# Scan constants and first chunks kept in tensors across stages, and the gate product one pair later in the second scan

## The chip, the cores and the metric

One core of one Trainium2 chip. The metric is the device time of the whole kernel in microseconds, the median of the runs.

## The reference

```
x = x + tanh(g_xattn) * SSM(ctx, layernorm(x))
x = x + tanh(g_ffn)  * Layer(layernorm(x))

# SSM, per batch of 1024 tokens and 1024 channels, 16 states per channel
u = silu(conv4(in_proj_w @ ctx) + conv_b)
dt_lo, B, C = split(x_proj_w @ u)
delta = softplus(dt_proj_w @ dt_lo + dt_proj_b)
state[t] = state[t-1] * exp(delta[t] * A) + delta[t] * u[t] * B[t]
y[t] = sum_n state[t, n] * C[t, n] + D * u[t]
y = y * silu(z)

# Layer: only the 128 tokens of a batch that a router scores highest (of all four batches: 512 rows)
h = rms_norm(rows); causal attention, 16 heads; MLP silu(h @ w_gate) * (h @ w_up) @ w_down
```

There are four batches; x is 4 x 1024 x 1024 and all is in float32.

## The kernel before

The kernel runs seven stages, one after the other: `project_stage`, `scan_stage(0)`, `route_stage(0)`, `layer_stage(0)`, `scan_stage(2)`, `route_stage(2)`, `layer_stage(2)`. The number is the first batch of the pair that the stage handles. Each stage has tensors and semaphores of its own, which are given back when it ends, and it ends with a barrier of all engines. SP waits, as a stage's last act, for the DMAs that it and ACT issued in it.

**Projection (line 59).** 32 steps, one for each batch and each of 8 groups of 128 channels (`e`). PE multiplies the context by in_proj, VectorE runs the convolution and ACT the silu; ACT stores the group's u and its gate input (silu of the normed x, 1 MB together) to a scratch tensor `ug` (line 194), and each batch's dt, B and C rows to a scratch tensor `xd` (line 202). SP loads x tile after tile (`load_x`, line 110), each when the tile before has been used.

**Scan (line 278).** The work is 32 units: 2 batches x 2 halves of 512 tokens (a chunk is one batch's half) x 8 channel groups. A unit has 16 states, in 8 pairs and 4 quads:

- ACT, `exp(delta * A)`, two per pair, into the PSUM ring `pA` (line 773). It also copies the transposed result of the unit before, `copy_x2`, from PSUM (line 698) at pair `X2_AT` = 4, and turns the gate (line 694).
- POOL, quads `x = du * bB` (line 531), and for pairs 2 and 5 the product with C (line 538), 
- VectorE, the 16 scans (line 823), the products with C for the other pairs (line 808), and the gate product (line 797) for the unit before. Its place is after pair `GATE_AT` = 1; it waits for PE's last sum of the unit before (`summed`) and for the turned gate.
- PE, sums of the states over pairs by products with the identity (line 592) into the PSUM tile `py`, the skip D * u (line 586, a product with the diagonal `diagD`), which for unit s begins when the gate product of s-1 has read `py`, and the product that adds x (lines 581 and 582). In program order it is skip(s), sums of pair 0, pair 1, then the add of unit s-1.
- SP loads `bB` (B of a chunk, broadcast to 128 partitions, 4 slices of 1 MB, line 421), `bC` (line 434), `dt` (412), `u` (386), the gate input and x (394, 398).

At its start the stage loads tanh inputs, `ssm`, `w_dt`, then dt, u, B and C of its first chunk; it makes the identity on POOL, tanh and the diagonals on ACT (line 765), and `negA`, minus the exp of A_log.

In the second scan (`fill=True`) PE also computes gate, up and down products of the MLP of the first pair of batches, between its sums, from a ring of four weight tiles (line 442), and VectorE and ACT carry its activations (lines 829 to 841). PE's order is fixed, so a product whose weights are late holds all that stands behind it.

**Layer (line 1127).** PE multiplies the selected rows with tiles of weights of 512 KB that SP loads into a ring of `SLOTS_W` = 8 slots, in the order wq 16 tiles, wk 8, wv 8 (from tile `T_V` = 24), wo 16 (line 1240). A tile's load waits until the tile whose slot it takes has been used. The DMA queue of SP works in order.

Some constants of the scan stage:

```
GATE_AT, ADD_AT, TURN_AT, DT_AT = 1, 1, 3, 5
READ_AT, X2_AT, COPY_AT = 1, 4, 6
```

Of the kernel before, what the change touches and what calls it, by code (L numbers as in the profile page):

```python
# [24 lines left out]
P = 128  # L25
# [33 lines left out]
def project_stage(nc, t, ctx):  # L59
# [31 lines left out]
    exponent = sem("exponent")  # L91

    with nc.Block() as block:
        @block.sync
        def _(sp):
# [73 lines left out]
        def _(act):  # L169
# [91 lines left out]
GATE_AT, ADD_AT, TURN_AT, DT_AT = 1, 1, 3, 5  # L261
# [16 lines left out]
def scan_stage(nc, t, ctx, first, fill):  # L278
# [10 lines left out]
    bB = sb("bB", [P, NS, HALF])  # L289
    bC = sb("bC", [P, NS, HALF])  # L290
# [19 lines left out]
    g_in, small, made, act_chain, consts = (sem(n) for n in ("g_in", "small", "made", "act_chain", "consts"))  # L310
# [1374 lines left out]
```

## Time and profile before

| | us |
|---|---|
| median of 3 runs | 3162.67 |
| lowest and highest | 3158.97, 3163.16 |
| the profiled execution | 3152.81 |
| its span (first to last instruction) | 3151.1 |

| engine | busy us | share of the span |
|---|---|---|
| PE (TensorE, products) | 2432.4 | 77% |
| VectorE (DVE) | 2176.0 | 69% |
| POOL (GpSimd) | 1668.0 | 53% |
| ACT (ScalarE) | 1288.0 | 41% |

The mean granted clock of PE is 0.858 of full. A profile gives the time of one execution; its span is 1.7 us short of that execution's time. The busy share is an average over seven stages with different limits, so it is read stage by stage: the rows below give the busy time of each engine in windows that begin and end with the stages. A row of the timeline says when an instruction began, how long it took, and in brackets how long its engine was idle before it and what ended that.

### The profile page before, as it was taken

The numbers are of one execution on the slowest core, as the hardware profiler recorded it, in microseconds if no ns is written. First come the engines' busy times: TensorE is split into PE (matmuls) and PEld (weight loads), VectorE is DVE, ScalarE is ACT, GpSimd is POOL, SyncE is SP. The second block draws the span as 40 slices with busy tenths as digits, with TensorE's granted clock in tenths as the row PEclk, the third lists the DMA queues.
The fourth block names the chain that finished last, engine by engine and source line by source line (L and its number), as shares of the span: only waits on it lengthen the run. The fifth ranks groups of instructions, "written<-read, shape, count | busy, mean of one in ns | idle before, by whom it ended". The sixth has DMA issues, their size and how long they took to land. (4 is left out here: it accounts for less than half of the span.)

```text
span 3151.1 us, 30288 instructions
## 1 busy us (share of the span) xinstructions
PE 2432.4 (77%) x10552; PEld 1700.3 (54%) x10552; DVE 2176.0 (69%) x2674; ACT 1288.0 (41%) x2311; POOL 1668.0 (53%) x601
## 2 busy tenths in 40 slices
PE   8996667666666632998488888888887179999998
PEld 3332555554545521854366676665554166658863
DVE  5664999999999985331599999999997832410000
ACT  4555555555555522131456555555543211510000
POOL 0001999999999941000688988899996000000000
PEclk9998677777777765999699998899998589999999
DMA  7545314114141134423623632633531564044443
GB/s 283 191 186 202 89 40 148 41 41 149 47 135 55 37 124 185 127 87 98 213 85 99 208 101 80 204 105 109 185 101 60 211 211 134 15 147 151 151 152 107
DMA packets 198094, 401.37 MB, mean 127 GB/s; under 512 B 16960, under 2 KB 85056, under 8 KB 192832
## 3 DMA queue, kind: packets, MB, share of 16 engines
q1 hardware_dynamic: 186752, 343.43, 34.8%
q10 hardware_dynamic: 9856, 51.38, 4.0%
q0 software_dynamic: 1344, 4.72, 0.4%
q8 instruction: 82, 1.34, 0.2%
q14 instruction: 60, 0.49, 0.0%
HBM read 323.98 MB, written 75.50 MB: 127 GB/s over the span
## 5 line engine op out<-in xcount | busy, mean ns | idle before, releaser
L531 POOL TENSOR_TENSOR s_x<-s_du,s_bB 128x2048 f32<-128x2048 f32 x256 | 1156.9, 4533 | 116.6 <-PE s_py L592 93.6
L592 PE MATMUL s_py<-s_ident,s_x 128*128 128x128 f32 x4096 | 668.4, 322 | 363.9 <-DVE s_x L808 351.7
L592 PEld LDWEIGHTS s_py<-s_ident,s_x 128*128 128x128 f32 x4096 | 583.2, 169 | 535.5 <-DVE s_x L808 431.8
L773 ACT ACTIVATE s_pA<-s_delta,s_negA 128x512 f32<-128x512 f32 x1024 | 666.1, 680 | 388.0 <-DVE s_x L808 381.7
L823 DVE TENSOR_TENSOR_SCAN s_pA<-s_pA,s_x 128x512 f32<-128x512 f32 x384 | 452.4, 1214 | 66.9 <-POOL s_x L531 46.7
L823 DVE TENSOR_TENSOR_SCAN s_pA<-s_pA,s_carry,s_x 128x512 f32<-128x512 f32 x384 | 471.6, 1270 | 0.1
L808 DVE TENSOR_TENSOR s_x<-s_pA,s_bC 128x1024 f32<-128x1024 f32 x384 | 461.9, 1203 | 1.0 <-DMA s_bC<-scratch_xd 0.9
L1324 PE MATMUL l_p<-l_hT,l_ring 128*128 128x256 f32 x1792 | 396.7, 380 | 1.8 <-ACT l_hT L1428 1.0
L1324 PEld LDWEIGHTS l_p<-l_hT,l_ring 128*128 128x128 f32 x1792 | 341.7, 191 | 49.5 <-issue 1.4
L538 POOL TENSOR_TENSOR s_x<-s_hp,s_bC 128x1024 f32<-128x1024 f32 x128 | 301.6, 2356 | 12.0 <-DVE s_hp L823 12.0
L1292 POOL TENSOR_TENSOR l_squares<-l_squares,l_minus_half 128x1 f32<-128x1 f32 x4 | 2.2, 554 | 494.6 <-DVE l_squares L1583 494.6
L151 PE MATMUL p_x<-p_ctxT,p_w_in 128*128 (+1 forms) x512 | 231.0, 604 | 9.4 <-DMA p_ctxT<-in_ctxT 9.3
L1331 PE MATMUL l_p<-l_ring,l_hidden 128*128 128x512 f32 x512 | 220.2, 592 | 0.0
L239 DVE SCALAR_TENSOR_TENSOR p_ug<-p_raw,p_conv,p_ug 128x1024 f32<-128x1024 f32 x96 | 123.3, 1285 | 87.1 <-ACT p_ug L185 78.5
L1301 POOL DMA_INDIRECT out_dram<-l_rows,l_row_i x2 | 1.9, 951 | 330.5 <-DVE l_rows L1610 330.5
L712 ACT ACTIVATE s_carry<-s_pA 128x2 f32<-128x2 f32 x192 | 33.1, 172 | 343.4 <-DVE s_x L808 343.4
L151 PEld LDWEIGHTS p_x<-p_ctxT,p_w_in 128*128 128x128 f32 x512 | 95.7, 192 | 143.4 <-issue 142.5
L1331 PEld LDWEIGHTS l_p<-l_ring,l_hidden 128*128 128x128 f32 x512 | 97.1, 190 | 121.1 <-issue 121.0
L823 DVE TENSOR_TENSOR_SCAN s_hp<-s_pA,s_carry,s_x 128x512 f32<-128x512 f32 x128 | 162.4, 1269 | 0.0
L125 POOL TENSOR_TENSOR p_rstd<-p_mv,p_minus_half 128x1 f32<-128x1 f32 x32 | 18.4, 575 | 262.4 <-DVE p_mv L234 262.4
L1605 DVE TENSOR_TENSOR l_hidden<-l_silu,l_p 128x256 f32<-128x256 f32 x32 | 13.5, 421 | 207.8 <-PE l_p L1324 207.8
L823 DVE TENSOR_TENSOR_SCAN s_hp<-s_pA,s_x 128x512 f32<-128x512 f32 x128 | 154.5, 1207 | 0.1
(177 smaller groups left out, 3034.8 us busy)
## 6 DMA issues: line engine op xcount, KB each, us to landing
scratch_ug<-p_ug ACTq DMA_DIRECT2D x32, 1024.0 KB, 3.9
s_bB<-scratch_xd SPq DMA_DIRECT2D x32, 1024.0 KB, 13.1
s_bC<-scratch_xd SPq DMA_DIRECT2D x32, 1024.0 KB, 14.0
p_xz<-in_x SPq DMA_DIRECT2D x32, 512.0 KB, 3.5
s_u<-scratch_ug SPq DMA_DIRECT2D x64, 256.0 KB, 3.6
s_gy<-scratch_ug SPq DMA_DIRECT2D x64, 256.0 KB, 4.2
s_xt<-in_x SPq DMA_DIRECT2D x64, 256.0 KB, 4.6
scratch_x<-s_xt SPq DMA_DIRECT2D x64, 256.0 KB, 4.3
```

What stands on the lines that cost most here:

```text
L125: pool.tensor_tensor(out=rstd[:, e % 2:e % 2 + 1], in0=mv[:, e % 2, 1:2], in1=minus_half[:], op=ALU.pow).then_inc(rstd_ready, 1)
L151: last = nc.tensor.matmul(halves(ps[e % 2], h), w_in[:, c, e * P:(e + 1) * P], ctxT[:, bass.ds((b * NK + c) * L + h * HALF, HALF)], start= ...
L239: nc.vector.scalar_tensor_tensor(out=ug[:, j, 0], in0=raw[:, j, i:i + L], scalar=conv[:, e, i:i + 1], in1=ug[:, j, 0], op0=ALU.mult, op1=A ...
L531: pool.tensor_tensor(out=x[:, 4 * g:4 * g + 4], in0=du[:, s % 2:s % 2 + 1].broadcast_to([P, 4, HALF]), in1=bB[:, 4 * g:4 * g + 4], op=ALU. ...
L538: pool.tensor_tensor(out=x[:, 2 * i:2 * i + 2], in0=hp[:, POOL_PAIRS.index(i)], in1=bC[:, 2 * i:2 * i + 2], op=ALU.mult).then_inc(pool_hc, 1)
L592: last = nc.tensor.matmul(py[:, a], x[:, n, a * P:(a + 1) * P], ident[:], is_transpose=True, start=False, stop=is_last and a == HALF // P - 1)
L712: nc.scalar.activation(kept, pA[:, j:j + 2, HALF - 1], ACT.Copy).then_inc(carried, 1)
L773: nc.scalar.activation(pA[:, n % 4], delta[:, s % 2], ACT.Exp, scale=negA[:, s % NE, n:n + 1]).then_inc(dA_ready, 1)
L808: nc.vector.tensor_tensor(x[:, 2 * i:2 * i + 2], pA[:, j:j + 2], bC[:, 2 * i:2 * i + 2], ALU.mult).then_inc(vec_hc, 1)
L823: nc.vector.tensor_tensor_scan(out, pA[:, n % 4], x[:, n], initial, ALU.mult, ALU.add).then_inc(scanned, 1)
L1324: last = nc.tensor.matmul(out[:, 0:ROWS], w[:, c * P:(c + 1) * P], src[:, c], start=c == 0, stop=c == KT - 1)
L1331: last = nc.tensor.matmul(banks[2 * a + h][:], src[:, a * P:(a + 1) * P], w[:, h * HALF:(h + 1) * HALF], start=is_first, stop=is_last)
```

## The change

Three parts.

1. A class `Kept` holds B, C, dt, u of one chunk, and the constants `ssm`, `w_dt`, `negA`, `diagD`, the identity and tanh(g), in tensors that live over the first five stages. `project_stage` loads the constants (after its first x loads), makes the identity and the diagonals, and after its last x load issues 11 loads of the first chunk: u twice (256 KB each), dt (64 KB), B and C (8 x 1 MB). SP waits for them at the end of the stage.
2. `layer_stage(0)` issues the same 11 loads for batch 2, after the load of tile 24. For the room its ring has 6 slots, not 8, and four of its work tensors share one. `scan_stage` has no loads, waits or making of constants at its start any more; its first loads are the gate input and x, and in the second scan then h2T, the coefficients and the weight ring. `negA` is computed in the first scan alone.
3. `GATE_AT` becomes (1, 2): in the second scan the gate product stands after pair 2.

```diff
+class Kept:
...
+    def load_units(self, sp, t, b, sem):
+        for e in range(2):
+            sp.dma_start(self.u[:, e], t["ug"][(b * NE + e) * P:(b * NE + e + 1) * P, 0:HALF]).then_inc(sem, 16)
+
+    def load_chunk(self, sp, t, b, sem):
+        sp.dma_start(self.dt[:, 0], t["xd"][b * ND:b * ND + NR, 0:HALF]).then_inc(sem, 16)
+        for g in range(NS // 4):
+            for dst, at in ((self.bB, b * ND + NR + 4 * g), (self.bC, b * ND + NR + NS + 4 * g)):
+                sp.dma_start(dst[:, 4 * g:4 * g + 4], t["xd"][at:at + 4, 0:HALF].partition_broadcast(P)).then_inc(sem, 16)
...
             with sp.Fori(1, NB) as b:
                 load_x(b, 0)
+            for e in range(2):
+                sp.wait_ge(ug_out[e], 16 + 16)
+            keep.load_units(sp, t, 0, kept)
+            sp.wait_ge(xd_out, 32 + 32)
+            keep.load_chunk(sp, t, 0, kept)
+            sp.wait_ge(kept, 16 * KEPT_LOADS)
             sp.wait_ge(xd_out, 32 * NB + 32)
...
             batch(0, True)
+            act.wait_ge(small, 48)
+            act.wait_ge(made, 2)
+            nc.scalar.activation(keep.tg[:], keep.tg[:], ACT.Tanh).then_inc(kept_chain, 1)
+            for e in range(NE):
+                last = nc.scalar.activation(keep.diagD[:, e], keep.ident[:], ACT.Copy, scale=keep.ssm[:, e, NS + 1:NS + 2])
+            last.then_inc(kept_chain, 1)
...
-GATE_AT, ADD_AT, TURN_AT, DT_AT = 1, 1, 3, 5
+GATE_AT, ADD_AT, TURN_AT, DT_AT = (1, 2), 1, 3, 5
...
-            sp.dma_start(tg[:], t["g"].partition_broadcast(P)).then_inc(g_in, 16)
-            sp.dma_start(ssm[:], t["ssm"].rearrange("(e p) c -> p e c", p=P)).then_inc(small, 16)
-            sp.dma_start(w_dt[:], t["w_dt"].rearrange("(e r) c -> r e c", r=NR)).then_inc(small, 16)
-            load_dt(0)
-            load_u(0)
-            load_B(0, 0)
-            load_C(0, 0)
-            load_u(1)
-            for g in range(1, QUADS):
-                load_B(0, g)
-                load_C(0, g)
             load_end(0)
...
-                    if i == GATE_AT and s:
+                    if i == GATE_AT[fill] and s:
                         gate(s - 1)
...
-    SLOTS_W = 8
+    SLOTS_W = 8 if last_half else 6
...
             for n in range(SLOTS_W, TILES):
                 load(n)
+                if n == T_V and not last_half:
+                    keep.load_units(sp, t, SPAN, kept)
+                    keep.load_chunk(sp, t, SPAN, kept)
```

VectorE's order in the second scan, pairs 0 to 3 of one unit (`s_pA` and `s_hp` are the outputs of scans, `s_x` the states' products with C, `s_gy` the gate's output). Before:

```order
L823 SCALAR_TENSOR_TENSOR s_pA<-s_pA,s_x 128x512 [waits s0_dA_ready]
L808 TENSOR_TENSOR s_x<-s_pA,s_bC 128x1024 [waits s0_scanned]
L823 SCALAR_TENSOR_TENSOR s_pA<-s_pA,s_x 128x512 [waits s0_dA_ready]
L797 TENSOR_TENSOR s_gy<-s_py,s_gy 128x512 [waits s0_gate_turned,s0_summed]
L823 SCALAR_TENSOR_TENSOR s_hp<-s_pA,s_x 128x512 [waits s0_pool_hc,s0_carried,s0_dA_ready,s0_w_ready]
L808 TENSOR_TENSOR s_x<-s_pA,s_bC 128x1024 [waits s0_scanned]
L823 SCALAR_TENSOR_TENSOR s_hp<-s_pA,s_x 128x512 [waits s0_dA_ready]
L823 SCALAR_TENSOR_TENSOR s_pA<-s_pA,s_x 128x512 [waits s0_dA_ready] x2
```

Changed:

```order
L841 SCALAR_TENSOR_TENSOR s_pA<-s_pA,s_x 128x512 [waits p_kept_chain]
L826 TENSOR_TENSOR s_x<-s_pA,k_bC 128x1024 [waits s0_scanned]
L841 SCALAR_TENSOR_TENSOR s_pA<-s_pA,s_x 128x512 [waits p_kept_chain]
L841 SCALAR_TENSOR_TENSOR s_hp<-s_pA,s_x 128x512 [waits s0_pool_hc,s0_carried,p_kept_chain,s0_w_ready]
L826 TENSOR_TENSOR s_x<-s_pA,k_bC 128x1024 [waits s0_scanned]
L841 SCALAR_TENSOR_TENSOR s_hp<-s_pA,s_x 128x512 [waits p_kept_chain]
L815 TENSOR_TENSOR s_gy<-s_py,s_gy 128x512 [waits s0_gate_turned,s0_summed]
L841 SCALAR_TENSOR_TENSOR s_pA<-s_pA,s_x 128x512 [waits p_kept_chain] x2
```

The gate product (line 797, 815 in the changed kernel) moved behind two scans and a product with C; all else keeps its place.

SP's queue where the projection ends and the first scan begins (`scratch_xd` holds dt, B and C rows, `scratch_ug` u and the gate input). Before, from the projection's last row; three more pairs of B and C loads with a u between the first two follow ahead of `s_gy`:

```order
L93 UNCONDITIONAL_BRANCH
L377 UNCONDITIONAL_BRANCH
L453 DMA s_tg<-in_g 128x2
L454 DMA s_ssm<-in_ssm 128x8x18
L455 DMA s_w_dt<-in_w_dt 32x8x128
L412 DMA s_dt<-scratch_xd 32x512
L386 DMA s_u<-scratch_ug 128x512
L421 DMA s_bB<-scratch_xd 128x4x512
L434 DMA s_bC<-scratch_xd 128x4x512
```

Changed, from the end of the x loop:

```order
L79 DMA k_u<-scratch_ug 128x512 x2
L82 DMA k_dt<-scratch_xd 32x512
L85 DMA k_bB<-scratch_xd 128x4x512
L85 DMA k_bC<-scratch_xd 128x4x512
...
L125 UNCONDITIONAL_BRANCH
L420 UNCONDITIONAL_BRANCH
L436 DMA s_gy<-scratch_ug 128x512
L440 DMA s_xt<-in_x 128x4x128
```

The loads of u, dt, B and C moved from behind the barrier of the scan stage to the end of the projection, and three more pairs of B and C follow there.

SP's queue in the layer stage of the first half. Before:

```order
L1240 DMA l_ring<-in_wk 128x1024 x8
L1240 DMA l_ring<-in_wv 128x1024 x8
L1240 DMA l_ring<-in_wo 128x1024 x9
L1253 DMA scratch_k<-l_kT 128x2048
L1256 DMA scratch_v<-l_v 128x2048
```

Changed:

```order
L1257 DMA l_ring<-in_wq 128x1024 x16
L1257 DMA l_ring<-in_wk 128x1024 x8
L1257 DMA l_ring<-in_wv 128x1024
L79 DMA k_u<-scratch_ug 128x512 x2
L82 DMA k_dt<-scratch_xd 32x512
L85 DMA k_bB<-scratch_xd 128x4x512
L85 DMA k_bC<-scratch_xd 128x4x512
...
L1257 DMA l_ring<-in_wv 128x1024 x7
L1257 DMA l_ring<-in_wo 128x1024 x7
```

Eleven loads now stand between the first and the second v tile; of B and C the first pair is shown here, and three more follow ahead of the seven v tiles.

## Rows read from the trace of the kernel before

**Rows 1.** Windows: length, busy (x) of PE, PEld, DVE, ACT, POOL, clock, DMA, GB/s

```profile
0.00:293.50 293.50, 263.87 (x640) 102.14 (x640) 175.59 (x290) 146.33 (x134) 18.69 (x37) 0.98 0.56 212
293.50:311.50 18.00, 6.16 (x12) 2.77 (x12) 0.00 (x0) 10.45 (x22) 7.50 (x5) 0.50 0.80 252
311.50:1143.30 831.80, 548.55 (x2608) 423.07 (x2608) 825.22 (x736) 449.94 (x821) 797.25 (x254) 0.74 0.26 76
1236.80:1500.70 263.90, 222.38 (x900) 155.07 (x900) 75.40 (x248) 57.58 (x175) 7.11 (x12) 0.93 0.37 119
1500.70:1517.30 16.60, 6.16 (x12) 2.77 (x12) 0.00 (x0) 10.45 (x22) 7.53 (x5) 0.50 0.88 248
1562.60:2431.00 868.40, 747.07 (x3779) 549.25 (x3778) 827.96 (x758) 469.90 (x856) 766.11 (x244) 0.93 0.39 121
```

**Rows 2.** Timeline, front of the first scan: start, duration, engine, line, [idle before]

```profile
298.01 0.43 SPq L421 DMA_DIRECT2D s_bB<-scratch_xd  x1
...
299.60 2.04 PE L564 MATMUL s_pm<-s_dt,s_w_dt 32*128 32x512 f32 x2 [8.91 <-DMA s_dt<-scratch_xd]
...
311.57 3.46 DVE L823 TENSOR_TENSOR_SCAN s_pA<-s_pA,s_x 128x512 f32<-128x512 f32 x3 [24.01 <-POOL s_x L531]
...
324.43 4.52 POOL L531 TENSOR_TENSOR s_x<-s_du,s_bB 128x2048 f32<-128x2048 f32 x1 [2.54 <-DMA s_bB<-scratch_xd]
...
335.55 1.23 DVE L823 TENSOR_TENSOR_SCAN s_pA<-s_pA,s_x 128x512 f32<-128x512 f32 x1 [3.70 <-ACT s_pA L773]
```

**Rows 3.** Timeline, front of the second scan, VectorE

```profile
1517.35 3.46 DVE L823 TENSOR_TENSOR_SCAN s_pA<-s_pA,s_x 128x512 f32<-128x512 f32 x3 [22.21 <-POOL s_x L531]
...
1552.45 1.23 DVE L823 TENSOR_TENSOR_SCAN s_pA<-s_pA,s_x 128x512 f32<-128x512 f32 x1 [14.09 <-ACT s_pA L773]
```

**Rows 4.** By tile and line: count, ns min/median/max, first and last start

```profile
L110 SPq DMA_DIRECT2D p_xz<-in_x x30: 327/332/348, 25.5 to 270.0; - x30
...
L194 ACTq DMA_DIRECT2D scratch_ug<-p_ug x32: 338/338/389, 28.1 to 288.9; - x32
...
L765 ACT ACTIVATE s_diagD<-s_ident,s_ssm x16: 384/384/385, 304.4 to 1512.2; 128x128 f32<-128x128 f32 x16
```

**Rows 5.** Layer stage, first half: timeline of SP and PE, one window

```profile
1256.65 3.64 PE L1313 MATMUL l_p<-l_ident,l_normed_rows 128*128 128x128 f32 x16 [23.00 <-ACT l_normed_rows L1421]
...
1326.93 27.52 SPq L1240 DMA_DIRECT2D l_ring<-in_wv  x8
...
1335.00:1358.60 23.60, 23.47 (x101) 18.86 (x100) 7.87 (x20) 2.55 (x6) 0.00 (x0) 1.00 0.43 134
...
1355.19 27.63 PE L1331 MATMUL l_p<-l_ring,l_hT 128*128 128x512 f32 x64
```

**Rows 6.** Waits, second scan (1550 to 2412 us); us in total, times, longest

```profile
DVE s_gy L797 <- PE s_py L592: 31.0, 16, 3.8
```

**Rows 7.** Timeline, second scan, a unit whose gate product does not wait

```profile
2406.39 0.67 DVE L797 TENSOR_TENSOR s_gy<-s_py,s_gy 128x512 f32<-128x512 f32 x1
...
2412.70 0.60 ACT L698 ACTIVATE s_xt<-s_pm 128x512 f32<-128x512 f32 x1 [0.77 <-PE s_pm L582]
...
2415.23 1.30 ACT L773 ACTIVATE s_pA<-s_delta,s_negA 128x512 f32<-128x512 f32 x2 [1.94 <-DVE s_x L808]
...
2416.31 1.25 DVE L823 TENSOR_TENSOR_SCAN s_hp<-s_pA,s_carry,s_x 128x512 f32<-128x512 f32 x1
```

**Rows 8.** Timeline, second scan, a unit whose gate product waits

```profile
2380.16 0.69 DVE L797 TENSOR_TENSOR s_gy<-s_py,s_gy 128x512 f32<-128x512 f32 x1 [2.74 <-PE s_py L592]
...
2387.09 0.60 ACT L698 ACTIVATE s_xt<-s_pm 128x512 f32<-128x512 f32 x1 [0.86 <-PE s_pm L582]
...
2390.10 1.25 DVE L823 TENSOR_TENSOR_SCAN s_hp<-s_pA,s_carry,s_x 128x512 f32<-128x512 f32 x1
```

**Rows 9.** Timeline, PE after idle, first and second scan

```profile
1120.88 2.04 PE L586 MATMUL s_py<-s_diagD,s_u 128*128 128x128 f32 x8 [3.39 <-DVE s_gy L797]
...
1640.82 1.09 PE L592 MATMUL s_py<-s_ident,s_x 128*128 128x128 f32 x8 [3.05 <-DVE s_x L808]
```

More of the change, by code:

```diff
@@ L90, in project_stage @@
     ug_out = [sem(f"ug_out{j}") for j in range(2)]
-    exponent = sem("exponent")
+    exponent, small, made, kept, kept_chain = (sem(n) for n in ("exponent", "small", "made", "kept", "kept_chain"))
     with nc.Block() as block:
@@ L120, in _ @@
             pool.memset(minus_half[:], -0.5).then_inc(exponent, 1)
+            pool.memset(keep.ident[:], 0.0).then_inc(made, 1)
+            pool.wait_ge(made, 1)
+            pool.affine_select(out=keep.ident[:], in_=keep.ident[:], compare_op=ALU.not_equal, fill=1.0, base=0,
+                               pattern=[[-1, P]], channel_multiplier=1).then_inc(made, 1)
             pool.wait_ge(exponent, 1)
@@ L275, with scan_stage @@
 WEIGHTS_AT = (0, 2, 5)
-def scan_stage(nc, t, ctx, first, fill):
+def scan_stage(nc, t, ctx, keep, first, fill):
     def sb(name, shape):
@@ L509, in _ @@
         def _(pool):
-            pool.memset(ident[:], 0.0).then_inc(made, 1)
-            pool.wait_ge(made, 1)
-            pool.affine_select(out=ident[:], in_=ident[:], compare_op=ALU.not_equal, fill=1.0, base=0,
-                               pattern=[[-1, P]], channel_multiplier=1).then_inc(made, 1)
             def begin(s):
@@ L526, in quad @@
                     pool.wait_ge(du_ready, s + 1)
-                if s % NE == 0:
-                    pool.wait_ge(B_in[g], 16 * chunk(s) + 16)
+                if s and s % NE == 0:
+                    pool.wait_ge(B_in[g], 16 * chunk(s))
                 if s:
@@ L557, in dt_proj @@
             def dt_proj(s):
-                if s % NE == 0:
-                    pe.wait_ge(dt_in[chunk(s) % 2], 16 * (chunk(s) // 2) + 16)
+                if s and s % NE == 0:
+                    pe.wait_ge(dt_in[chunk(s) % 2], 16 * ((chunk(s) + 1) // 2))
                 if s == 1:
@@ L760, in _ @@
             softplus_ln(0)
-            act.wait_ge(act_chain, 2)
-            nc.scalar.activation(negA[:], negA[:], ACT.Copy, scale=-1.0).then_inc(act_chain, 1)
-            act.wait_ge(made, 2)
-            for e in range(NE):
-                last = nc.scalar.activation(diagD[:, e], ident[:], ACT.Copy, scale=ssm[:, e, NS + 1:NS + 2])
-            last.then_inc(consts, 1)
-            act.wait_ge(act_chain, 3)
+            if first == 0:
+                act.wait_ge(act_chain, 1)
+                nc.scalar.activation(negA[:], negA[:], ACT.Copy, scale=-1.0).then_inc(act_chain, 1)
+                act.wait_ge(act_chain, 2)
             for s in range(UNITS):
@@ L804, in times_C @@
                 j = 2 * (i % 2)
-                if s % NE == 0 and i == min(m for m in VEC_PAIRS if m // 2 == i // 2):
-                    dve.wait_ge(C_in[i // 2], 16 * chunk(s) + 16)
+                if s and s % NE == 0 and i == min(m for m in VEC_PAIRS if m // 2 == i // 2):
+                    dve.wait_ge(C_in[i // 2], 16 * chunk(s))
                 dve.wait_ge(scanned, NS * s + 2 * i + 2)
@@ L1617, with run @@
 SCRATCH_KIND = "Internal"
-STAGES = ((project_stage,), (scan_stage, 0, False), (route_stage, 0), (layer_stage, 0),
-          (scan_stage, SPAN, True), (route_stage, SPAN), (layer_stage, SPAN))
+STAGES = ((project_stage,), (scan_stage, 0, False), (route_stage, 0), (layer_stage, 0), (scan_stage, SPAN, True))
+LAST_STAGES = ((route_stage, SPAN), (layer_stage, SPAN))
 def build(nc, t):
-    for stage, *which in STAGES:
-        with nc.cleanup_on_exit(), ExitStack() as ctx:
-            stage(nc, t, ctx, *which)
+    def run(stages, keep):
+        for stage, *which in stages:
+            with nc.cleanup_on_exit(), ExitStack() as ctx:
+                stage(nc, t, ctx, keep, *which)
+    with ExitStack() as outer:
+        run(STAGES, Kept(nc, outer))
+    run(LAST_STAGES, None)
 def kernel(x, ctx_1024, g_xattn, g_ffn, L0_xattn_in_proj_w, L0_xattn_conv_w, L0_xattn_conv_b, L0_xattn_x_proj_w,
```

89 lines of the change are left out of this document (46 added, 43 removed).

## The prediction

> **What bounds the kernel now.** I read the busy time by stage first [rows 1]. In the projection (0 to 293.5 us) TensorE is busy for 263.9 of 293.5 us. In the layer stage of the first half (1236.8 to 1500.7) it is busy for 222.4 of 263.9. In both scans VectorE is the bound: 825.2 of 831.8 us in the first, 828.0 of 868.4 in the second. So the first scan has 6.6 us of slack and the second some 40. Between projection and first scan, and between layer stage and second scan, lie two fronts of 18.0 and 16.6 us in which VectorE does nothing: these the change shortens. What it adds is load traffic at the end of the projection and in the layer stage, and there the question is whether TensorE's work covers it.
>
> Then the timeline of the first front [rows 2]. PE waits 8.91 us for the data of its dt_proj product (over the stage's change); the product starts at 299.60 and the first scan at 311.57, so 11.97 us of dependent work (softplus on ACT, two POOL products, one POOL quad) follow. The B and C loads issued from 298.01 end with the quad at 324.43, which waited for its slice of B. VectorE's 3.70 us stall at 335.55 comes of the same late loads. At the second front [rows 3] the first scan starts at 1517.35, and a long stall of 14.09 us at 1552.45 follows: PE, in order, waits for the first gate weights, which stand behind the same loads in SP's queue, and with it the next unit's exps.
>
> **The change part by part.**
>
> *First front.* The 11 kept loads (u, dt, B, C of the first chunk) are 2 x 0.25 + 0.06 + 8 x 1 = 8.56 MB. They are put behind the last x load, which is issued at 270.0 [rows 4]; ACT's tanh and eight diagD copies (384 ns each in the scan stages, and overlapping, so some 2.4 us for eight [rows 4], of which I put 1.9 on the path, since ACT hands PE its next tile) push that to 271.9. Their duration: in the front 7.25 MB (four slices of B, three of C, one of u) took from 298.01 to 324.43, 26.4 us, so 3.64 us per MB [rows 2]; 8.56 MB are 31.2 us. Three of the 32 gate/u stores of 1 MB (the last issued at 288.9, one per step of 8.1 us [rows 4]) share the queue time: 3 x 3.64 = 10.9. The stage now ends when SP has seen its kept loads land: 271.9 + 31.2 + 10.9 = 314.0 in place of 295.3. From there 12.2 us (the 11.97 and a short start) to the first scan: 326.2 against 311.57, **+14.6**. The 3.70 us stall goes, since B and C are all there: **-3.7**. Sum **+10.9**. Bounds: with the transfers all hidden the stage starts at 295.3, so -4.1, and the stall goes: -8; with a rate a tenth lower than in the front, +14.
>
> By the Trainium skill ("DMA: Bandwidth & Descriptors", Where 436 GB/s comes from) transfers between HBM and SBUF are bound by some 358 GB/s of HBM per core; 8.56 MB would take 25 us rather than 31.2, and the sum would be about 6 us smaller in each of the two stages. The trace has 288 GB/s for this very pattern of loads, so I stay with that.
>
> *Layer stage.* The kept loads of batch 2 are issued behind weight tile 24, the first v tile, and the ring has 6 slots, not 8. SP issues one tile per 3.9 us there (8 from 1326.93 over 27.5 us), so tile 24 now goes two tiles later, at about 1335 [rows 5]. The 31.2 us of kept loads end near 1366, and tile 25, next in the same queue, lands some 2 us after (0.5 MB at that rate), 1368. PE takes one v tile per 3.45 us from 1355.19 (64 products in 27.63), so it needs tile 25 at 1358.6. PE is busy 23.47 of the 23.60 us before that [rows 5], so there is no slack and it stalls 9.7 us. After an idle of 23.00 us its first 16 products of 128 columns took 3.64 us [rows 5], where 8 at the full clock take 1.09 [rows 9], and work goes at half rate for some 5 us: +2.4. Six ring loads instead of eight ahead of the gather of rows: up to 3.6 less by the same rate, I take 1.5. Sum **+11**; bounds 0 (tile 25 lands in time for another reason) and +14. That the ring has six slots costs nothing by itself: six tiles ahead are over 20 us of PE's work, against the 2 us that a tile needs at the front's rate. Were that cover gone, each later tile would cost what its load is late.
>
> *Second front.* Stage start 1500.7 to first scan 16.66 us becomes 12.2: **-4.4**. The gate weights' loads now stand behind four others alone (gate/u, x, h2T, coef), so the 14.09 us stall goes: **-14.1** [rows 3]. Sum **-18.5**, and the likeliest error is a remnant of 1 to 3 us, since h2T still stands ahead of them in the queue.
>
> *Gate product one pair later, second scan only.* It waits for PE's sums in 16 of 31 units, 31.0 us in all, 3.8 at most [rows 6]. Two scans and a C product more, 3.4 to 3.5 us, are put ahead of it, so nearly all of that ends: -31.0. Its followers, though, are a chain: gate product, skip product on PE, the add on PE, ACT's copy (line 698), and behind that copy in ACT's order the exps 10 and 11, which the scans need. In a unit without a wait [rows 7] the gate product starts at 2406.39, the copy at 2412.70 and ends at 2413.3, the exps start at 2415.23, the scan on them at 2416.31. Moved by 3.5 us the copy ends 2416.8 and the first exp 2417.5, so the scan is 1.2 us late. In a unit with a wait [rows 8] the product starts 2380.16 after 2.74; the others would start 2.74 sooner, but PE's own order holds the skip where it was, so the copy still ends 2387.69, the first exp 0.7 later at 2388.4; the scan of 2390.10 would be due at 2387.36: 1.05 us late. The same overlay over all 31 units gives stalls of 0.2 to 2.4 us, sum 29.5 (18 in the units with a wait, 11.5 in those without). So **-31.0 + 29.5 = -1.5**. Bounds -31 (no copy binds) and +25 (PE's slower clock in most units, below).
>
> *PE's clock.* In units without a wait PE would now idle 2 to 4 us ahead of the skip. In the first scan one such skip, after 3.39 us idle, took 2.04 us; in the second, sums after 3.05 us idle still ran 8 in 1.09 [rows 9]. The first scan grants 0.74 of the clock on average, the second 0.93 [rows 1]. With the skip, sums and add at half rate the chain is 1.9 us longer; I take 2 units, **+4**.
>
> The Trainium skill ("TensorE: Matmul & The Clock Gate", Part 1) says that the array falls back to half its clock when it idles. By that, with the idle stretches above, I would expect rather more than 2 units; it is the reason for a rival below, whose time is worked out from rows.
>
> Sum: 10.9 + 11 - 18.5 - 1.5 + 4 = **+5.9**. The profiled execution is 3152.8 us, which gives 3158.7; the median of the three times shown, 3162.67, is 9.9 above it, and the forecast for the median is 3162.67 + 5.9 = **3168.6**.
>
> **The rivals.**
>
> *A, the forecast:* +5.9, its own range -6 to +16 (load exposure 5 off either way, gate 5).
>
> *B, the copy does not hold the exps back:* the margin in the overlay is a few tenths to 1.5 us, and a scan can start on the first of two exps. Then the gate gives its -31 whole, and with the +4 of the clock the sum is 10.9 + 11 - 18.5 - 27 = -24, 3139. For it: the waits are a plain row; against it: the copy stands ahead of the exps in ACT's order in every unit.
>
> *C, slower, PE's clock falls in the units without a wait:* 15 units x 1.9 = 28.5 in place of 4, so +30.4, 3193. It decides from some six units with a skip at 2.04 us on: 6 x 1.9 is 11.4 in place of 4, which takes the sum to +13; at all 15 it is the full price. For it: the 3.39 us row; against: the 3.05 us row [rows 9], and the gate, up and down products that fill the second scan.
>
> *D, the kept loads are hidden:* if the end of the projection carries them (DMA there has room) and the v tiles come in time, 10.9 goes to -8 and 11 to +3: -8 + 3 - 18.5 - 1.5 + 4 = -21, 3142. Against it: 8.56 MB, 31 us, between 272 and 295.
>
> *E, the tails of the loads shift elsewhere and cancel:* the two late starts equal the two gains, and the gate stalls equal its waits, 0 within 6: 3163. Or the loads that are moved ahead are merely paid there and the gate's move is inert: then the change does not do what it says.
>
> **Numbers.** A measurement of this kernel tells about 0.2%, 6.3 us, from no change (3156.3 to 3169.0). Chances: A 0.40, B 0.19, C 0.14, D 0.14, E 0.13. Of A's own range -6 to +16 some 0.14 lies within 6 us, 0.25 above. So faster B + D + 0.01 = 0.34, same 0.13 + 0.14 = 0.27, slower 0.14 + 0.25 = 0.39. The range takes in B, D and all but the top of C: 3138 to 3192. A alone: 3157 to 3179.
>
> **What would show it.** First scan start at 326 and not below 312, with SP's last stage event 18 us later; no stall near 335 after it. Layer stage: PE idle of near 10 us behind the first v tile, released by the ring load. Second scan: first VectorE scan 12 us behind the stage's start, no 14 us stall. VectorE's waits for PE in the gate product near 0, and in their place some 30 us of waits of the scans for ACT's exps. If these are under 5 us, B. If the skip products are 2.04 us in ten units or more, C. If PE's idle behind the first v tile is under 3 us, or the first scan begins before 312, D. If the second scan from 1562.6 on still takes 868 us with no waits of either kind, the gate step is wrong.

## The result, and the profile after

| | before | changed |
|---|---|---|
| median, 5 runs each | 3159.71 us | 3180.48 us |
| lowest and highest | 3151.30, 3163.16 | 3174.24, 3185.90 |
| span of the profiled execution | 3151.1 | 3177.5 |

The ratio of the two is 1.0076, with a 95% interval of 1.0062 to 1.0090: the change makes the kernel 0.76% slower, 24 us (the two medians differ by 20.8). The forecast was slower too, by 5.9 us, and the range given, 3138 to 3192, holds the time; how much slower was not right. The two spans differ by 26.4 us.

Windows by stage in the changed kernel (length, busy us of PE, PEld, VectorE, ACT, POOL with counts, PE's clock, DMA share, GB/s); they answer to [rows 1].

```profile
0.00:298.50 298.50, 269.16 (x640) 104.27 (x640) 175.61 (x290) 148.87 (x143) 19.34 (x39) 0.96 0.59 220
...
298.50:330.10 31.60, 6.19 (x12) 2.77 (x12) 0.00 (x0) 8.02 (x13) 7.04 (x4) 0.50 0.68 210
...
330.10:1157.30 827.20, 552.13 (x2608) 425.40 (x2608) 824.97 (x736) 449.95 (x821) 797.06 (x254) 0.73 0.24 70
...
1527.30:1539.20 11.90, 6.19 (x12) 2.75 (x12) 0.00 (x0) 7.49 (x11) 6.99 (x3) 0.50 0.90 324
...
1539.20:1574.50 35.30, 22.02 (x120) 18.00 (x120) 35.04 (x33) 19.46 (x40) 35.14 (x12) 0.88 0.16 49
...
1574.50:2457.10 882.60, 761.04 (x3768) 562.38 (x3768) 824.76 (x753) 463.89 (x848) 763.52 (x243) 0.90 0.39 119
```

VectorE's busy time in the two scans has not changed. What has changed is how long the windows are. Laid end to end, from one landmark on VectorE to the next:

| stretch | before | changed | difference | forecast |
|---|---|---|---|---|
| start to first scan of the first scan stage | 311.57 | 330.13 | +18.6 | +14.6 |
| to its last gate product | 831.0 | 826.5 | -4.5 | -3.7 |
| to the start of the second scan stage | 358.1 | 370.6 | +12.5 | +11 |
| to its first scan | 16.7 | 12.0 | -4.7 | -4.4 |
| to its last gate product | 911.8 | 917.2 | +5.4 | -11.6 |
| to the end | 722.0 | 721.0 | -1.0 | 0 |

The last gate products are at 1142.58 and 2429.11 us before, 1156.65 and 2456.46 changed; the second scan stage starts at 1500.69 and 1527.27. Five of six rows are within 4 us of what was forecast. The second scan is 17 us off.

**The first front.** Timeline of the changed kernel at the end of the projection; the line answers to [rows 2, 4].

```profile
275.79 0.81 SPq L79 DMA_DIRECT2D k_u<-scratch_ug  x2
...
299.34 0.61 SPq L85 DMA_DIRECT2D k_bC<-scratch_xd  x1
...
294.14 0.34 ACTq L239 DMA_DIRECT2D scratch_ug<-p_ug  x1
...
318.16 2.04 PE L589 MATMUL s_pm<-k_dt,k_w_dt 32*128 32x512 f32 x2 [22.24 <-PEq L1647]
...
330.13 3.46 DVE L841 TENSOR_TENSOR_SCAN s_pA<-s_pA,s_x 128x512 f32<-128x512 f32 x3 [37.33 <-POOL s_x L556]
```

SP had all kept loads issued at 299.9. The stage starts at 318.1 (314 was forecast), 18 us after the last issue and 24 us after ACT's last store of gate and u: the transfers set it. PE's 22.24 us of idle and most of VectorE's 37.33 are this wait. The chain behind it took 12.0 us, for 12.2 forecast. There is no stall near 350 that would answer to the 3.70 us before.

The 4 us that the forecast is short here stand ahead of the transfers: the kept loads begin at 275.79 us where 271.9 was forecast, and from there to the stage's start it is 42.3 us, for 42.1 forecast. ACT's last store is 5.2 us later than before (294.14 for 288.90), and most of that comes of the diagonals. Rows of ACT and PE where batch 1 begins:

```profile
86.79 2.43 ACT L261 ACTIVATE k_diagD<-k_ident,k_ssm 128x128 f32<-128x128 f32 x8
...
97.98 1.98 PE L183 MATMUL p_xdp<-p_ug,p_w_x 128*64 128x512 f32 x4 [3.10 <-ACT p_xd L244]
...
99.88 9.14 PE L196 MATMUL p_x<-p_ctxT,p_w_in 128*128 x16
```

ACT's eight diagonals take 2.43 us ahead of the next group's copy; PE idles 3.10 us and then needs 9.14 us for 16 products, which took 7.13 before. 2.0 us more is what some 4 us at the lower clock level (1.2 GHz of 2.4) make. For the diagonals 1.9 us were put down, and the clock behind the idle was left out; diag_late below gives them 3.9. Another 1.2 us are lost before them: the product that PE begins at 86.74 us began at 85.52 in the kernel before. That start lies between 84.1 and 87.7 us in the traces of the experiments, so whether the change has a part in it is open.

**The layer stage.** SP and PE where the v tiles begin; they answer to [rows 5].

```profile
1348.48 0.33 SPq L1257 DMA_DIRECT2D l_ring<-in_wv  x1
...
1364.08 4.45 SPq L85 DMA_DIRECT2D k_bC<-scratch_xd  x1
...
1368.98 3.60 PE L1352 MATMUL l_p<-l_ring,l_hT 128*128 128x512 f32 x8
...
1383.86 16.59 PE L1352 MATMUL l_p<-l_ring,l_hT 128*128 128x512 f32 x34 [11.29 <-DMA l_ring<-in_wv]
```

Tile 24 was loaded at 1348.48, the last kept load issued at 1364.1 to 1368.5, and the second v tile came in at 1383.86. PE idled 11.29 us for it; 9.7 was the forecast, and with the clock 12.1, less 1.5. The 56 products behind the stall took 26.03 us, 1.9 more than at the rate of the kernel before (64 in 27.63), where 2.4 was forecast. The 1.5 us for fewer ring loads ahead of the gather of rows hardly came: PE's idle there fell from 23.00 to 22.74 us. In all it measured 12.5. The rest of the stage behind the v tiles is as before.

**The second front.** PE's first product, VectorE's first scan; they answer to [rows 3].

```profile
1527.31 2.04 PE L589 MATMUL s_pm<-k_dt,k_w_dt 32*128 32x512 f32 x2 [6.35 <-PEq L1647]
...
1539.28 3.46 DVE L841 TENSOR_TENSOR_SCAN s_pA<-s_pA,s_x 128x512 f32<-128x512 f32 x3 [17.15 <-POOL s_x L556]
```

From start to first scan 12.0 us in place of 16.7, and no stall of 14.09 us behind it: VectorE is busy for 35.04 of the next 35.30 us. This part came out within 0.3 us (-4.7 for -4.4, and the stall gone).

**The second scan.** The waits from 1577 to 2440 us (total, times, longest), answering to [rows 6].

```profile
ACT s_xt L719 <- PE s_pm L607: 119.8, 30, 6.0
...
PE s_py L611 <- DVE s_gy L815: 45.5, 23, 4.3
...
DVE s_hp L841 <- ACT s_pA L791: 36.5, 27, 3.1
...
DVE s_x L826 <- DMA k_bC<-scratch_xd: 6.7, 6, 1.9
...
DVE s_pA L841 <- ACT s_pA L791: 4.9, 6, 1.6
...
DVE s_swish L854 <- ACT s_sigmoid L754: 4.4, 8, 1.4
```

The waits of the gate product are gone (31.0 us), as forecast. In their place VectorE waits for ACT's exps. Counted over the whole second scan, its last unit too, these are 44.1 us in 34 waits, and there are two that the forecast left out: 6.7 us for slices of C, and the sigmoid's, up from 2.9 to 4.4. Two units show how the wait comes about. First one in which PE's skip runs at the full clock; they answer to [rows 7]:

```profile
2379.83 0.66 DVE L815 TENSOR_TENSOR s_gy<-s_py,s_gy 128x512 f32<-128x512 f32 x1
...
2380.64 1.13 PE L611 MATMUL s_py<-k_diagD,k_u 128*128 128x128 f32 x8 [1.40 <-DVE s_gy L815]
...
2386.13 0.60 ACT L719 ACTIVATE s_xt<-s_pm 128x512 f32<-128x512 f32 x1 [4.33 <-PE s_pm L607]
...
2387.34 1.28 DVE L841 TENSOR_TENSOR_SCAN s_hp<-s_pA,s_carry,s_x 128x512 f32<-128x512 f32 x1 [0.99 <-ACT s_pA L791]
```

The gate product starts at 2379.83, ACT's copy 6.3 us later, ends at 2386.73, and the scan behind the exps is 0.99 us late. In another unit PE idled 3.57 us before the skip:

```profile
2100.07 0.67 DVE L815 TENSOR_TENSOR s_gy<-s_py,s_gy 128x512 f32<-128x512 f32 x1
...
2100.88 2.04 PE L611 MATMUL s_py<-k_diagD,k_u 128*128 128x128 f32 x8 [3.57 <-DVE s_gy L815]
...
2107.97 0.60 ACT L719 ACTIVATE s_xt<-s_pm 128x512 f32<-128x512 f32 x1 [5.05 <-PE s_pm L607]
...
2109.38 1.22 DVE L841 TENSOR_TENSOR_SCAN s_hp<-s_pA,s_x 128x512 f32<-128x512 f32 x1 [2.43 <-ACT s_pA L791]
```

The eight products take 2.04 us, the sums behind them 1.75 rather than 1.04, and ACT's copy starts 7.9 us behind the gate product rather than 6.3. The scan is 2.43 us late. Of 31 units, 8 are of this kind (skip product of 1.45 us or more), with 19.2 us of waits for exps in all, 2.4 each. The other 23 have 24.9 us, 1.08 each. Forecast were 0.95 each, and two units at the lower clock. The 23 are of two kinds: in seven PE had not idled before the skip at all, but came to it 0.9 to 1.9 us after the gate product began, late by its own work, and these lost 1.6 us each (11.2 in all); the other 16 lost 0.86 each.

C's slices are late by SP's order: the load of u waits for the skip product and stands ahead of C's loads in the queue. The skip product is 3.5 us later in relation to the scans, and so are these.

```profile
1780.00 0.34 SPq L428 DMA_DIRECT2D k_u<-scratch_ug  x1
...
1781.40 1.00 SPq L474 DMA_DIRECT2D k_bC<-scratch_xd  x2
...
1788.73 1.22 DVE L826 TENSOR_TENSOR s_x<-s_pA,k_bC 128x1024 f32<-128x1024 f32 x1 [1.90 <-DMA k_bC<-scratch_xd]
```

### The profile page after: what moved, and what is told of

Its sections match the earlier page's. It is cut to its first block and busy times, and to the rows that moved or that the text cites. A ratio compares the mean times of both kernels' runs of the same rounds, so it can differ in the third digit from the quotient of the medians.

```text
span 3177.5 us, 30252 instructions
## 1 busy us (share of the span) xinstructions
PE 2456.0 (77%) x10552; PEld 1716.9 (54%) x10552; DVE 2177.0 (69%) x2674; ACT 1282.5 (40%) x2300; POOL 1667.3 (52%) x599
## 5 line engine op out<-in xcount | busy, mean ns | idle before, releaser
L556 POOL TENSOR_TENSOR s_x<-s_du,k_bB 128x2048 f32<-128x2048 f32 x256 | 1156.0, 4531 | 108.7 <-PE s_py L617 88.5
L617 PE MATMUL s_py<-k_ident,s_x 128*128 128x128 f32 x4096 | 676.3, 325 | 322.8 <-DVE s_x L826 315.5
L617 PEld LDWEIGHTS s_py<-k_ident,s_x 128*128 128x128 f32 x4096 | 594.2, 171 | 487.5 <-DVE s_x L826 379.8
L791 ACT ACTIVATE s_pA<-s_delta,k_negA 128x512 f32<-128x512 f32 x1024 | 665.9, 680 | 344.6 <-DVE s_x L826 335.6
L826 DVE TENSOR_TENSOR s_x<-s_pA,k_bC 128x1024 f32<-128x1024 f32 x384 | 461.7, 1202 | 7.1 <-DMA k_bC<-scratch_xd 7.0
L1345 PEld LDWEIGHTS l_p<-l_hT,l_ring 128*128 128x128 f32 x1792 | 340.2, 190 | 48.9 <-issue 1.4
L563 POOL TENSOR_TENSOR s_x<-s_hp,k_bC 128x1024 f32<-128x1024 f32 x128 | 301.8, 2358 | 21.3 <-DVE s_hp L841 21.3
L611 PE MATMUL s_py<-k_diagD,k_u 128*128 128x128 f32 x512 | 95.1, 344 | 94.5 <-DVE s_gy L815 90.6
L170 POOL TENSOR_TENSOR p_rstd<-p_mv,p_minus_half 128x1 f32<-128x1 f32 x32 | 18.6, 582 | 266.7 <-DVE p_mv L285 266.7
```

The lines of the kernel that those rows point to most:

```text
L556: pool.tensor_tensor(out=x[:, 4 * g:4 * g + 4], in0=du[:, s % 2:s % 2 + 1].broadcast_to([P, 4, HALF]), in1=bB[:, 4 * g:4 * g + 4], op=ALU. ...
L563: pool.tensor_tensor(out=x[:, 2 * i:2 * i + 2], in0=hp[:, POOL_PAIRS.index(i)], in1=bC[:, 2 * i:2 * i + 2], op=ALU.mult).then_inc(pool_hc, 1)
L611: last = nc.tensor.matmul(py[:, a], u[:, s % 2, a * P:(a + 1) * P], diagD[:, s % NE], start=a == 0, stop=False)
L617: last = nc.tensor.matmul(py[:, a], x[:, n, a * P:(a + 1) * P], ident[:], is_transpose=True, start=False, stop=is_last and a == HALF // P - 1)
L791: nc.scalar.activation(pA[:, n % 4], delta[:, s % 2], ACT.Exp, scale=negA[:, s % NE, n:n + 1]).then_inc(dA_ready, 1)
L826: nc.vector.tensor_tensor(x[:, 2 * i:2 * i + 2], pA[:, j:j + 2], bC[:, 2 * i:2 * i + 2], ALU.mult).then_inc(vec_hc, 1)
```

## The experiments

Each was timed together with the kernel before, whose median was 3155 to 3157 us there; so each is read by its ratio to it. The changed kernel's is 1.0076.

### gate_back: the gate product back after pair 1

```diff
-GATE_AT, ADD_AT, TURN_AT, DT_AT = (1, 2), 1, 3, 5
+GATE_AT, ADD_AT, TURN_AT, DT_AT = (1, 1), 1, 3, 5
```

> The changed kernel with the gate product of the second scan back after pair 1. Theory (the later gate product holds ACT's copy back, and the copy holds the exps): the second scan loses its 44 us of waits for exps and gets back some 31 us of gate waits, and the slow skips go; by the two traces the step cost 19.5 us, so about 3161 us, 17 to 20 below the changed kernel. Rival (the second scan is longer for the kept tensors or for the traffic of its loads, and the gate's place is innocent): within 5 us of the changed kernel, 3176 to 3185.

Measured: 3164.35 us, ratio 1.0029 (1.0014 to 1.0043), 15 us less than the changed kernel in ratio and 16 in medians, a little under the 17 to 20 expected. The second scan took 898.2 us from first scan to last gate product, 19.0 less than the changed kernel's 917.2 and 13.6 less than the 911.8 before, which is the 14.09 us stall. Waits, 1576 to 2440 us:

```profile
DVE s_gy L815 <- PE s_py L617: 33.7, 16, 4.0
...
DVE s_pA L841 <- ACT s_pA L791: 2.3, 5, 0.5
```

The gate waits are back (31.0 us before) and the 44 of exps gone, and so are the slow skips: none takes more than 1.13 us. The rest of the change, the kept tensors, costs 0.3% without the gate's move.

### gate_only: nothing but the gate product after pair 2, in the kernel before

```diff
-GATE_AT, ADD_AT, TURN_AT, DT_AT = 1, 1, 3, 5
+GATE_AT, ADD_AT, TURN_AT, DT_AT = (1, 2), 1, 3, 5
...
-                    if i == GATE_AT and s:
+                    if i == GATE_AT[fill] and s:
```

> The kernel before with one edit, the gate product of the second scan after pair 2. Theory: the step alone costs 17 to 20 us, so 3177 to 3180, with 0 to 3 us of gate waits and some 40 us of waits of scans for exps. Rival (the step is free, what costs is tied to the kept tensors): 3160 within 5.

Measured: 3173.05 us, ratio 1.0054 (1.0038 to 1.0070), 17 us slower than before, at the lower end of the 17 to 20 expected. From first scan to last gate product 931.8 us for 911.8. The waits in it:

```profile
PE s_py L586 <- DVE s_gy L797: 40.4, 17, 4.1
...
DVE s_hp L823 <- ACT s_pA L773: 39.5, 27, 3.4
...
DVE s_x L808 <- DMA s_bC<-scratch_xd: 7.0, 5, 1.9
```

The step costs its price by itself, and the late slices of C with it (7.0 us): they are no matter of the kept tensors. The rival is out.

### copy_later: ACT's copy behind exps 10 and 11 too

```diff
-READ_AT, X2_AT, COPY_AT = 1, 4, 6
+READ_AT, X2_AT, COPY_AT = 1, (4, 5), 6
...
-                    if i == X2_AT and s:
+                    if i == X2_AT[fill] and s:
```

> The changed kernel with ACT's copy of x (copy_x2) one pair later in the second scan too, behind exps 10 and 11. Theory (the copy's place ahead of the exps is the link): the 44 us of waits for exps fall below 12, PE's slow skips stay, and the time falls by 25 to 35, to about 3150. Rival (PE's lower clock is the link: the chain is late whatever stands behind the copy, and waits move to the next exps or to PE's turn of the gate): the time falls by less than 12, to 3168 to 3180.

Measured: 3162.69 us, ratio 1.0025 (1.0015 to 1.0035), 16 to 18 us less than the changed kernel. That lies between the two expectations. Waits:

```profile
PE s_py L611 <- DVE s_gy L815: 90.9, 28, 6.2
...
DVE s_pA L841 <- ACT s_pA L791: 20.4, 19, 2.2
...
DVE s_x L826 <- DMA k_bC<-scratch_xd: 11.5, 6, 3.9
```

The waits for exps fall from 44 to 23 us, not below 12. They are other waits now, nearly all in front of scans of `s_pA` rather than `s_hp`. The waits for C go up to 11.5. So part of them did move to the next exps, as the rival had it. PE waits for the gate product twice as long as in the changed kernel (45.5 us there), and of 31 skip products 21 now take 1.45 us or more, yet the scan is 16.7 us shorter. The copy's place ahead of the exps is the main link. But the lower clock is not free here either: 22.1 of the 23.4 us of waits for exps stand in the 21 units with slow skips, 1.05 us each, and 1.3 us in the ten others. By the same count a unit with a slow skip has 2.4 us in the changed kernel. These are counts by unit in one trace each; they show where the waits stand, not what they would be at full clock.

### diag_late: tanh and the diagonals behind the projection's loop

```diff
             batch(0, True)
-            act.wait_ge(small, 48)
-            act.wait_ge(made, 2)
...
             copy_out(NB - 1)
+            act.wait_ge(small, 48)
+            act.wait_ge(made, 2)
...
```

> The changed kernel with tanh and the eight diagonals of ACT moved behind the projection's loop, where ACT waits. Theory (ahead of batch 1 they cost 3.9 us of the projection, by the stall of PE and the clock after it, and all behind it moves with them): 3 to 5 us less, 3176, the last store of gate and u at 290 us rather than 294. Rival (the end of the stage is set by the kept loads, which do not move): within 1 us of the changed kernel's 3180.

Measured: 3175.15 us, ratio 1.0067 (1.0051 to 1.0084), 5 us less in medians and 3 in ratio; the intervals overlap, so the time alone doesn't settle it. The trace does:

```profile
290.31 0.34 ACTq L239 DMA_DIRECT2D scratch_ug<-p_ug  x1
...
294.18 2.44 ACT L264 ACTIVATE k_diagD<-k_ident,k_ssm 128x128 f32<-128x128 f32 x8
...
326.80 3.46 DVE L841 TENSOR_TENSOR_SCAN s_pA<-s_pA,s_x 128x512 f32<-128x512 f32 x3 [37.82 <-POOL s_x L556]
```

The last store is at 290.31 for 294.14, 3.8 us sooner, and the first scan at 326.80 for 330.13, 3.3 us sooner. The diagonals cost ACT 2.44 us where it waits anyway.

From the product ahead of the diagonals to the last store it is 207.4 us in the changed kernel (86.74 to 294.14) and 203.5 here (86.83 to 290.31), so the diagonals cost 3.9. How much of this is the clock can be read from the next run, spread_layer, which leaves them where they are. There PE idled as long and stayed at full clock:

```profile
96.98 1.08 PE L193 MATMUL p_xdp<-p_ug,p_w_x 128*64 128x512 f32 x4 [3.09 <-ACT p_xd L254]
...
97.99 7.13 PE L206 MATMUL p_x<-p_ctxT,p_w_in 128*128 x16
```

The same stretch took 206.1 us (85.74 to 291.85): 2.6 for the idle, and 1.3 for the clock where it fell.

### spread_layer: the kept loads of the layer stage behind every second tile

```diff
+            queued = [] if last_half else keep.loads(sp, t, SPAN, kept)
             for n in range(SLOTS_W, TILES):
                 load(n)
-                if n == T_V and not last_half:
-                    keep.load_units(sp, t, SPAN, kept)
-                    keep.load_chunk(sp, t, SPAN, kept)
+                if n % 2 == 0 and queued:
+                    queued.pop(0)()
```

Here `keep.loads` gives the same 11 loads as a list, to be issued one by one.

> The changed kernel with the 11 kept loads of the layer stage laid one behind every second weight tile from tile 6 on, not all behind tile 24. Theory (the cost in this stage is the tile queued behind 8.56 MB): the 11.3 us stall of PE at the second v tile goes, and with it the clock behind it, so 11 to 13 us less, about 3168. Rival (the extra traffic itself costs, whatever its place: two tiles and one kept load are 2 MB or 7.3 us for 7.8 us of PE's work, with a ring of six): the stall is split into several of 1 to 3 us and the time falls by less than 4.

Measured: 3168.58 us, ratio 1.0039 (1.0026 to 1.0052), 12 us less than the changed kernel. PE's v products, whole:

```profile
1368.11 27.63 PE L1362 MATMUL l_p<-l_ring,l_hT 128*128 128x512 f32 x64
```

There is no idle time in or ahead of them. From the first scan's last gate product to the second's first scan it is 370.0 us, for 382.6 in the changed kernel and 374.8 before: 12.6 us less, and all that the stage now differs from before is the front's gain of 4.7. The traffic costs nothing in this stage when it is spread, and 12.6 us in one piece.

### slots_alone: a ring of six slots, nothing else, in the kernel before

```diff
-    SLOTS_W = 8
     last_half = first + SPAN == NB
+    SLOTS_W = 8 if last_half else 6
```

> The kernel before with a ring of 6 slots in the layer stage of the first half, nothing else. Theory (six tiles ahead cover every load): within 3 us of the kernel before. Rival (the ring's depth is part of the cost of the layer stage): 5 or more slower, with waits of PE for l_ring.

Measured: 3154.15 us, ratio 0.9994 (0.9983 to 1.0005). The two slots cost nothing, and PE waits for no ring tile in that stage.

### spread_all: both sets of loads spread, diagonals late, gate product back

```diff
-            with sp.Fori(1, NB) as b:
-                load_x(b, 0)
...
+            queued = keep.loads(sp, t, 0, kept)
+            for b in range(1, NB):
+                for e in range(NE):
+                    sp.wait_ge(gate_ready, b * NE + e + 1)
+                    sp.dma_start(xz[:, e % 2], t["x"][b * L + e * P:b * L + (e + 1) * P, :]).then_inc(x_in[e % 2], 16)
+                    if b * NE + e >= NE + 3 and (b * NE + e) % 2 and queued:
...
+                        queued.pop(0)()
```

> The changed kernel with the gate product back after pair 1, the diagonals behind the loop, the layer stage's kept loads spread, and those of the projection one behind every second x tile of batches 1 to 3. Theory (hoisting the chunk is worth the two shorter fronts if the loads have cover): first scan near 307.5 us on VectorE, no stall near 335, second front 12 us without the 14 us stall; 16 + 5 + 12 + 19 below the changed kernel, 3128, and 27 below the kernel before of this job. Rival (the loads take their time from the projection wherever they stand: x tiles late, PE's clock down): the projection grows by 5 to 15 us, 3135 to 3145.

Measured: 3129.88 us, ratio 0.9920 (0.9902 to 0.9938), 25 us faster than the kernel before and 1.5% faster than the changed kernel. Timeline: the dt_proj product, VectorE's first scan in each stage, the last gate product of the second scan.

```profile
294.62 2.04 PE L605 MATMUL s_pm<-k_dt,k_w_dt 32*128 32x512 f32 x2 [5.37 <-PEq L1663]
...
306.59 3.46 DVE L857 TENSOR_TENSOR_SCAN s_pA<-s_pA,s_x 128x512 f32<-128x512 f32 x3 [20.46 <-POOL s_x L572]
...
1505.17 3.46 DVE L857 TENSOR_TENSOR_SCAN s_pA<-s_pA,s_x 128x512 f32<-128x512 f32 x3 [17.55 <-POOL s_x L572]
...
2408.86 0.69 DVE L831 TENSOR_TENSOR s_gy<-s_py,s_gy 128x512 f32<-128x512 f32 x1 [2.15 <-PE s_py L633]
```

The stage starts at 294.6 rather than 318.1 and its first scan is at 306.59, 5.0 us before that of the kernel before and 20.2 before diag_late's. So the projection carries 8.56 MB of loads with no loss, given 8.1 us steps and one load in two of them. There is no stall behind either front. Its second scan, 903.7 us, is 5.5 longer than gate_back's 898.2, by gate waits of 39 us for 34; why these differ between two kernels with the same order was not tried.

### spread_copy_later: as spread_all, with the gate product after pair 2 and the copy later

It differs from spread_all by the edits of copy_later and the changed kernel's `GATE_AT`.

> As spread_all, but with the gate product after pair 2 and ACT's copy after exps 10 and 11. By the two second scans measured (898 us with the gate product back, 900 with the copy later) it is 2 us slower than spread_all, within 6 either way. Rival (with both moves VectorE gains over the gate product after pair 1, since its gate waits are gone): 8 or more faster.

Measured: 3131.56 us, ratio 0.9920 (0.9907 to 0.9933). The same as spread_all, as expected. From 1540 to 2400 us the gate product has no wait for PE, for 36.9 us in spread_all, and in their place 22.8 us of waits for exps and 11.1 for C, for 2.3 and 0.8. In the traces the second scan is 5.3 us shorter (898.4 us for 903.7); the times do not show it.

### fill_late: two more MLP products ahead of the skip

```diff
-FILL = (2, 2, 3, 3, 3, 3, 4, 5)
+FILL = (2, 2, 3, 3, 2, 3, 3, 7)
```

> The changed kernel with the MLP's products shared out otherwise over PE's slots of a unit: (2, 2, 3, 3, 2, 3, 3, 7) for (2, 2, 3, 3, 3, 3, 4, 5), so two more stand ahead of the skip product, where PE idled 3.6 us in the units with slow skips. Theory (eight of 31 skips at the lower clock make 10 of the 44 us of waits for exps): at most two slow skips are left, and the time falls by 5 to 12. Rival (the lower clock is a by-product, the copy's place is all): slow skips go, the waits stay at 40 or more, the time within 3 us of the changed kernel's 3180. A second way to fail: PE is now late for the gate product, whose waits come back.

Measured: 3184.74 us, ratio 1.0085 (1.0071 to 1.0100), no faster than the changed kernel, if anything slower. The attempt does not tell the theories apart. Slow skips fell only from 8 to 6, waits for exps were 48.9 us, and in several units PE now came to the skip 1.7 to 2.8 us after the gate product, late by its own work, so that the chain was as long as before without any lower clock: nine such units lost 2.2 us each, the six with slow skips 2.4. So a unit loses about as much where PE is late by its own work as where it is late by its clock. The second way to fail that was named (PE late) is what happened, though the gate product itself did not wait.

### fill_late_best: the same sharing out in spread_all

> spread_all with the same sharing out of the MLP's products. The gate product stands after pair 1 there and waits for PE's sums, 34 us in all; two products more ahead of the skip cannot help it, and one that stands before pair 7's sums could make it later. Theory: 3128 to 3136, no faster. Rival: PE's sums of pairs 4 to 6 come sooner for one product fewer ahead of them, gate waits fall by 5 or more, 3125 or less.

Measured: 3144.92 us, ratio 0.9956 (0.9940 to 0.9971), 15 us slower than spread_all where at most 6 was expected. VectorE's waits in the gate product went from 17 to 24 in number and the last gate product from 2408.86 to 2421.18, of which 0.5 us are from before the second scan. The order of the MLP's products in a unit is not free to move.

## Why the prediction was right or wrong

- **The side and the range** were right: slower, within 3138 to 3192. The size, +5.9, was a quarter of the 24 us.
- **First front, +10.9 of both terms.** Measured +18.6 - 4.5 = +14.1. The mechanism (the stage ends when its loads have landed) was right and its size 3.2 us short. The term that was too small is "of which I put 1.9 on the path": the diagonals cost 3.9, of which 1.3 is the clock after PE's idle of 3.10 us. 1.2 us more were lost before them, by what is open, and the transfers took 42.3 us for 42.1. spread_all shows that the loads themselves needn't have been exposed.
- **Layer stage, +11.** Measured +12.5, of it 11.29 a single wait. spread_layer takes 12.6 off by the place of the loads alone, so this reading is shown. That six slots cost nothing was shown by slots_alone; they gave nothing back either (PE's idle before the first products of the stage is 22.55 us there for 23.00), so the -1.5 for them has no run behind it.
- **Second front, -18.5.** Measured -4.7 and the stall of 14.09 gone, -18.8 (the stall is 13.6 by gate_back against before). Right.
- **Gate product, -1.5 and +4 for the clock.** Measured +19.5 by the two traces (the 17 us by which the second scan misses the forecast, and the 2.5 of these two terms), 19.0 by gate_back, 20.0 in the trace and 17 us in time by gate_only. This is the step that failed, not in its mechanism but in its size. The waits did change places: -31.0 and, for exps, +41.8 net, not 29.5 + 4. By the counts of the units: had the eight units with the lower clock lost 1.08 us like the rest, their 19.2 us would be 8.6, so the clock is worth about 10.6 us, where "I take 2 units" gave 4. This split is worked out from one trace; fill_late, meant to test it, did not. The other 4 us or so stand in the seven units in which PE came late by its own work (1.6 us each), a case that the overlay did not have; in the 16 that it describes it had 0.95 and 0.86 were measured. The remaining 6.5 us are C's slices and 1.5 the sigmoid, which the forecast left out: "who is queued behind the skip on SP" was not asked. 41.8 + 6.5 + 1.5 - 31.0 = 18.8 of the 19.5.
- **Rival B**, that the copy doesn't bind, is out by the 44 us of waits for exps and by copy_later, which gives 16 to 18 us back by moving the copy. **Rival C**, the clock in 15 units, is half true: 8 units, at some 1.3 us each (2.4 less 1.08) rather than 1.9. The row that spoke against it (a sum at full clock after 3.05 us idle) was one place; seven skips after idles of 3.29 us and more ran slow, an eighth after 2.42, and one after 3.04 us ran fast. **Rival D** did not happen, but spread_all is what it would have been. **Rival E**, that the two fronts cancel, has some truth: all but the gate is +14.1 + 12.5 - 4.7 - 14.1 - 1.0 = +6.8 of the 26.4 us, and gate_back measured +9.

What stays open is how much of the gate step's cost would be left if PE never fell to its lower clock; the experiment for it changed PE's load as well. With the copy moved too, nearly all waits for exps that are left stand in units with slow skips, so the clock may be worth more than the 10.6 us above.

## What to carry to other kernels

A hoisted load is not hidden because an engine is busy; it has to fit between the transfers that this engine is waiting for. The same 8.56 MB cost 12.6 us as one piece in the queue ahead of a weight tile and nothing as one load per two tiles, and the start of a stage 20 us or nothing. A wait on one engine is not a gain to be had by moving the waiting instruction: ask what its result releases, two or three engines on, and what stands in line behind that: here 31 us of waits became over 50. And an idle stretch in front of PE can cost twice, by its length and by the slower work behind it: here 2.6 us, and 1.3 more in the run in which the clock fell.

## What was not expected of the hardware

- More work at the lower PE clock did not mean a longer scan. In copy_later 21 of 31 skip products took 1.47 to 2.05 us instead of 1.13, PE waited 91 us for gate products, and the scan was 16.7 us shorter than the changed kernel's with its 8. What the slow skips still cost there stands in 22.1 us of waits for exps.
- After 3.10 us of idle in the projection 16 products took 9.14 us instead of 7.13. After 3.09 us at the same place in spread_layer they took 7.13. In the second scan the eight of a skip ran in 1.13 us after 3.04 us of idle, and in 2.02 us after 2.42; ahead of that one PE had idled 3.16 us at 2143 us and worked at the lower clock until 2155. The length of the last idle stretch alone did not tell which it would be.
- The Trainium skill ("DMA: Bandwidth & Descriptors", Where 436 GB/s comes from) gives some 358 GB/s as the bound between HBM and SBUF for one core. In the second front of the changed kernel the DMA engines moved 324 GB/s at a busy share of 0.90. The 11 kept loads of the layer stage and the tile behind them, 9.06 MB (of 1024 KB each), took from 1348.85 to 1383.86, 35.0 us or 271 GB/s; with what else was under way the core moved 311 GB/s there, its DMA engines busy 0.99 of the time:

```profile
1348.85:1383.86 35.01, 23.59 (x101) 18.60 (x99) 7.88 (x20) 2.48 (x6) 0.00 (x0) 0.90 0.99 311
```

Both stretches stay below the page's figure. For this pattern of loads the 3.64 us per MB measured before were the better number, and even a little low (3.86 here).
